# Two steps of a linear-attention round trade places: level product and X-transposed product on TensorE, their sums on VectorE

## What is computed

```python
def step(carry, inp):
    s, mem = carry
    qt, kt, vt, sdt, abt, bbt = inp
    mem = DECAY * mem + sdt
    hard = (mem > THR)                       # spikes; mem is lowered by THR where one fell
    ...
    s = s * alpha[..., None]                 # decay gate, per key channel
    u = jnp.einsum('bhd,bhdv->bhv', kt, s)
    s = s - beta[..., None] * jnp.einsum('bhd,bhv->bhdv', kt, u)
    s = s + beta[..., None] * jnp.einsum('bhd,bhv->bhdv', kt, vt)
    out = jnp.einsum('bhdv,bhd->bhv', s, qt)
    return ((s, mem), out)
...
y = x + y @ w_out * gate
y = y + silu(h2 @ w_ff1) * (h2 @ w_ff3) @ w_ff2
# then cross attention over 77 context rows, and a feed-forward part with signs as weights
```

## Time and profile before

| | |
|---|---|
| median of 3 runs | 1113.32 us (1108.06 to 1115.84) |
| the profiled execution | 1114.58 us, its span 1112.8 us |
| PE busy | 976.0 us (88%) |
| PE weight loads busy | 653.3 us (59%) |
| DVE busy | 699.5 us (63%) |
| ACT busy | 481.1 us (43%) |
| POOL busy | 210.5 us (19%) |

### The profile page before, as it was taken

The page is one execution under the profiler, slowest core; times in us unless marked ns, Lnnn a source line. Parts: engine busy times, 40 slices in busy tenths (PEclk is TensorE's granted clock), DMA queues, the critical chain, the costliest instruction groups (busy, mean ns, idle before and its releaser), DMA issues. The chain is left out here.

```text
span 1112.8 us, 40031 instructions
## 1 busy us (share of the span) xinstructions
PE 976.0 (88%) x16710; PEld 653.3 (59%) x16710; DVE 699.5 (63%) x2510; ACT 481.1 (43%) x1378; POOL 210.5 (19%) x394
## 2 busy tenths in 40 slices
PE   6888769999999999999999888689799899899896
PEld 2332347777777777777777776365446446446442
DVE  2886886988888888889776664146235425524710
ACT  7667312555555555555555555213124323323311
POOL 7100200212222122122122211222101111210300
PEclk8989955999999999999999999789899999899999
DMA  3000000000000000000001000400001000000100
GB/s 95 1 0 1 1 2 3 4 4 4 4 4 4 4 5 4 4 4 5 4 4 29 4 4 4 130 10 23 0 1 29 14 1 21 21 1 4 30 0 10
DMA packets 18652, 13.83 MB, mean 12 GB/s; under 512 B 2491, under 2 KB 17259, under 8 KB 18475
## 3 DMA queue, kind: packets, MB, share of 16 engines
q1 hardware_dynamic: 18475, 11.28, 3.5%
HBM read 7.70 MB, written 1.05 MB: 8 GB/s over the span
## 5 line engine op out<-in xcount | busy, mean ns | idle before, releaser
L935 PE MATMUL banks<-work 64*64 64x64 f32 x3072 | 98.5, 234 | 26.2 <-DVE gates L674 13.0
L994 PE MATMUL banks<-work 64*64 64x32 f32 x2560 | 108.1, 224 | 6.4 <-ACT work L1351 5.0
L1285 ACT COPY work<-banks 128x128 f32<-128x128 f32 x160 | 43.1, 269 | 160.2 <-PE banks L970 160.0
L199 DVE SCALAR_TENSOR_TENSOR gates<-mom,gates 128x16 f32<-128x16 f32 x512 | 100.6, 196 | 9.5 <-ACT gates L1258 4.5
L203 DVE SCALAR_TENSOR_TENSOR mom<-gates 128x16 f32<-128x16 f32 x512 | 102.8, 201 | 5.0
L994 PEld LDWEIGHTS banks<-work 64*64 64x64 f32 x2560 | 92.8, 139 | 19.0 <-issue 10.9
L637 DVE COPY_PREDICATED gates<-work,banks 128x256 f32<-128x256 uint32 x192 | 102.0, 531 | 1.1
L935 PEld LDWEIGHTS banks<-work 64*64 64x64 f32 x3072 | 73.3, 139 | 44.6 <-issue 21.4
L531 POOL TENSOR_TENSOR mom<-mom 128x4 f32<-128x4 f32 x32 | 7.2, 226 | 386.5 <-ACT work L1330 386.5
L608 DVE TENSOR_TENSOR work<-work 128x256 f32<-128x256 f32 x160 | 67.8, 424 | 19.5 <-PE banks L935 18.5
L647 DVE TENSOR_TENSOR work<-work,banks 128x128 f32<-128x128 f32 x160 | 45.6, 285 | 50.1 <-PE banks L994 47.0
(11 more groups left out here) (256 smaller groups left out, 2141.5 us busy)
## 6 DMA issues: line engine op xcount, KB each, us to landing
work<-gates SPq DMA_DIRECT2D x28, 38.5 KB
qT<-in_x_dram SPq DMA_DIRECT2D x4, 256.0 KB, 4.1
work<-in_x_dram SPq DMA_DIRECT2D x4, 256.0 KB, 2.8
out_dram<-work SPq DMA_DIRECT2D x4, 256.0 KB, 2.3
gates<-in_w_ff_dram SPq DMA_DIRECT2D x3, 256.0 KB, 3.4
wv_sb<-in_wv_dram SPq DMA_DIRECT2D x1, 512.0 KB, 5.0
work<-in_w_out_dram SPq DMA_DIRECT2D x1, 512.0 KB, 4.1
gates<-in_x_Wq_dram SPq DMA_DIRECT2D x1, 512.0 KB, 5.4
```

Of the source, the lines that this page charges most:

```text
L199: ve.scalar_tensor_tensor(mem[:, :, t], neg_mem, -0.9, mem[:, :, t], ALU.mult, ALU.add).then_inc(charged, 1)
L935: last = pe.matmul(level_out(l)[to, a], KS[rows, n.two, hp], late[rows, hp], start=True, stop=True)
L994: last = pe.matmul(packed(psXT, l)[rows, a], Z[rows, l - 1, z], second_half(XT[:, n.two], l)[rows, a], start=True, stop=True)
L1285: ac.copy(first_half(Z[:, l - 1], l), packed(psZX_half, l)).then_inc(z_ok, 1)
```

## The change

In four of the five steps of a body, l = 1, 2, 3 and 5, TensorE's `level(aft, l)` goes ahead of `make_xt(nxt, l)`. VectorE's `add_xt(nxt, l)` goes from in front of `prefix(aft, l)` to behind `suffix(aft, l)`, still ahead of `keep(aft, l)`. Step 4 stays as it was. No instruction is added or removed.

```diff
@@ VectorE's body
                         spike(scan, h + 1)
-                        if nxt:
+                        if nxt and l == 4:
                             add_xt(nxt, l)
                         if l == 4 and gate:
                             drive(gate)
@@
                         spike(scan, h + 3)
                         if aft:
                             suffix(aft, l)
+                        if nxt and l != 4:
+                            add_xt(nxt, l)
                         spike(scan, h + 4)
                         if aft:
                             keep(aft, l)
@@ TensorE's body
                         if l == 4 and gate:
                             spike_sums(gate)
-                        if nxt:
+                        if nxt and l == 4:
                             make_xt(nxt, l, gate, gate_old)
                         if l == 4 and gate and gate.n > HP:
                             spike_counts(gate, aft)
                         if aft:
                             level(aft, l, gate, gate_old)
+                        if nxt and l != 4:
+                            make_xt(nxt, l, gate, gate_old)
                         if l == 3 and cur:
                             correct(cur)
```

## The result

| | before | changed |
|---|---|---|
| median | 1110.71 us (4 runs) | 1131.91 us (4 runs, 1127.59 to 1133.49) |
| ratio | | 1.0179, 95% interval 1.0127 to 1.0231 |
| profiled execution, span | 1112.8 us | 1130.9 us |

A forecast was written before the change was run, and what follows sets the result against it. TensorE and VectorE were both nearly full, bound by chains of waits between them. Losses of 7.8 (steps 1 to 3), 4.4 (step 5), 1.4 and 3.0 us (other bodies) sum to 16.6, giving 1130 us; range 1118 to 1140.

The forecast's parts named there:

- The first rival: Waits ahead of `add_xt(1)` and `prefix(5)`: both vanish, 0.57 us off each of 22 bodies, 1101 us; chance 0.07.
- the one that nothing changes: Whole kernel: TensorE overlaps `make_xt` and the level product in either order, 1113 us; chance 0.03.
- Step 1: `level(1)` ahead of `make_xt(1)`: `level(1)` some 0.2 us earlier, `add_xt` takes 0.20 back, `level(2)` gains 0.09 us.
- Step 2: `make_xt(2)` behind `level(2)` loses the wait for `keep(1)` that covered it: `make_z(3)` 0.13 us late.
- Step 3: `make_xt(3)` no longer fills the wait for `beta`: `correct` 0.31 us late in 15 bodies, 0.45 in 7; 7.8 us.
- GpSimd's hold: VectorE's spike held beside GpSimd's `keys`, late by step 1: 0.20 us in 16 of 22 bodies, 1133 us; chance 0.16.
- Step 5: End of body: `add_xt(5)` delays `keep(5)`, and level 0 waits for it: 0.20 us a body, 4.4 us in 22.
- the ring: Level product, `prefix`, `suffix`, `keep`, next level product: said to set the time in steps 1 and 2.
- The side sum for TensorE: End of body: with `make_xt(5)` queued behind `level(5)`, TensorE reaches level 0 at 417.45 instead of 417.35.
- The swallowed lateness: Wait for `alpha` in step 5 absorbs the 0.31 to 0.45 us of steps 1 to 3: 1122 us; chance 0.22.
- The other bodies: Four bodies with gates and no spikes lose 1.4 us in all; five with neither lose 0.6 each, 3.0.
- the upper bound: `make_xt` behind the level product costs its whole 0.63 us: `correct` 0.62 late, 0.96 a body, 1141 us.

The follow-up runs named there:

- step 2 alone: Kernel before with both halves of the change (TensorE's and VectorE's reordering) in step 2 only: 1.0106 of before.
- step 1 alone: Kernel before with both halves of the change in step 1 only: 1.0016 of before, interval holding 1.
- VectorE's half: Kernel before with only `add_xt` moved behind `suffix` in steps 1, 2, 3 and 5, TensorE's order as before: 1.0209 of before.
- the run with `add_xt` behind `keep`: Kernel before with the change in step 5 only, but `add_xt(5)` placed behind `keep(5)`: 1.0005 of before.
- TensorE's half alone: Kernel before with only the level product ahead of `make_xt` in steps 1, 2, 3 and 5, `add_xt` still ahead of `prefix`: 1.0621, 1179.6 us.
- split keys with step 1: Kernel before with GpSimd's `keys` as four instructions of one head pair each, plus both halves of the change in step 1: 1.0029 of before.
- steps 1 to 3: Kernel before with both halves of the change in steps 1, 2 and 3, step 5 as before: 1.0139 of before.
- step 3: Kernel before with both halves of the change in step 3 only: 1.0073 of before.
- step 5 (both ways): Kernel before with the change in step 5 only: `add_xt(5)` ahead of `keep(5)` 1.0042 of before, behind it 1.0005.
- split keys alone: Kernel before with GpSimd's `keys` as four instructions of one head pair each, same result: 0.9965 of before.
- short keys: GpSimd's `keys` computes one head pair of four, output not the reference's: 0.9966 of before in the old order, 1.0138 in the changed order.

## Why the prediction was right

**The sum.** 1130 us were forecast, 1.015 of the median then known; measured are 1131.9 and 1.0179. The rise itself was forecast as 16.6 us; it is 18.1 between the profiled executions and 21.2 between the medians, since the median of before fell to 1110.7 with a fourth execution. That 1130 came so close is in part that luck. The first rival (1101) and the one that nothing changes are out. The order of the parts was right, their sizes partly by luck, as follows.

**Step 1** was right to 0.02 us in the body walked: `level(1)` at 2.73, `keep(1)` at 4.20 (forecast 4.19), `level(2)` at 5.07 (5.06). TensorE's `make_z(2)` was 0.15 us late, not 0.20.

**Step 2** and its lost cover: `make_z(3)` 0.09 to 0.16 us late (forecast 0.13). The run of step 2 alone shows the step to be a loss.

**Step 3** was right in kind and too high for that body, too low for the mean. `correct` was 0.21 us late in the body walked, forecast 0.31: `make_xt` behind the level product took 0.33 us up to `correct`, and only up to `turn_out` the 0.39 of the sum. But most bodies are not that one. I had given 7 of 22 to the wait for `beta`; in the changed kernel the wait is in 13 places. The walk did say that `make_xt` fills the wait for `beta`, but it let `beta` "move little", and in 13 bodies `beta` is late by the hold; without cover all of that lateness comes through. In the mean of the 20 bodies `correct` is 0.46 us late (0.36 by the sum), `alpha` 0.54, and with the 0.20 of step 5 that is the 0.74 us a body, not the 0.55 of the sum: 14.8 us in 20 bodies instead of 11.1. The term of steps 1 to 3 is the one that was mis-sized.

**GpSimd's hold**, the rival of 0.16, came in addition: 13 bodies held ahead of `keep(2)` instead of 6. Its price measured with the short instruction is 0.10 us a body, where the rival had 0.15 (3.3 us over 22). Its path was another: the rival had `keys` late by step 1, but step 1 alone took the hold away from `keep(2)`, and step 2 alone brought it to 11 bodies, since `add_xt(2)` puts the spike inside `keys`.

The rule of the Trainium skill, "SBUF — State Buffer", section "Who interferes with whom", is borne out: what has two inputs in SBUF was held beside `keys` (a spike, and in the run of VectorE's half `suffix`), and what reads PSUM and SBUF was not. The section also says that the order of issue decides which of the two blocks, so that GpSimd can be the one held; the prediction left this out, and the last paragraph of this text has it. In the changed kernel one `add_xt` starts inside `keys` and takes its usual 0.28 us:

```profile
237.19 0.74 POOL L506 TENSOR_TENSOR work<-kT,gates 128x256 f32<-128x256 f32 x1
237.24 0.28 DVE L647 TENSOR_TENSOR work<-work,banks 128x128 f32<-128x128 f32 x1
```

**Step 5** was right: 0.20 us, end 2.05 us, and it is the ring. The side sum for TensorE (417.45) was too high, since it gave `read_chunk` its whole length of 1.05 us; the run with `add_xt` behind `keep` had level 0 start 0.88 us after it.

**The swallowed lateness** (0.22) did not come: `level(5)` is as late as `correct`, in the walked body 0.25 against 0.21 us.

**The other bodies**: with gates alone 1.3 us, forecast 1.4. Without gates 4.3 us in four, where 0.6 each, 2.4, was forecast; the granted clock, next but one section, has part in the excess. **What made the sum come out** is also the start: the two bodies ahead of the first mark were forecast to lose 1.1 us, and the stage was 3.0 us shorter in the profiled execution. That is scatter of single executions as far as the runs show: the first mark lies between 190.6 and 200.4 us in the 14 traces, and in those with the old order in all steps at 193.6, 196.3 and 198.0. Without it the forecast would have been some 4 us further off, still inside the range.

Two smaller slips: at the upper bound `correct` is 0.55 us late by the prediction's own terms (0.31 + 0.24), not 0.62, which moves the 1141 by some 1 us; and the 0.70 for slower is more than the 0.52 and 0.16 that it is made of.

## What to carry to other kernels

A wait that is taken away from one engine can be worth nothing, as here, if the work that stood in another engine's wait loses its place. Ask of each moved step both what it waited for and whose wait it was filling, and put work that nobody waits for behind the step that somebody does: the same `add_xt` cost 0.20 us a body ahead of `keep` and nothing behind it. An order on two engines is one choice, not two: TensorE's half alone cost over three times what both cost together (6.2% against 1.8%), and VectorE's half alone as much as both (2.1%).

## What the runs showed of the hardware

**The granted clock.** TensorE's granted clock has a part in the result, and the prediction had left it out. Stretches of the kernel before (columns as in the earlier trace rows: busy us of PE, PEld, DVE, ACT and POOL; then the granted clock as a share of 2.4 GHz, the DMA share and GB/s):

```profile
180.00:185.00 5.00, 5.00 (x122) 4.13 (x125) 3.12 (x14) 1.11 (x3) 1.18 (x2) 0.50 0.02 3
630.00:640.00 10.00, 8.59 (x317) 6.98 (x312) 7.30 (x23) 4.91 (x21) 3.34 (x9) 1.00 0.02 6
```

The same stretches of the changed kernel:

```profile
180.00:185.00 5.00, 4.51 (x134) 3.54 (x132) 4.96 (x22) 0.90 (x3) 2.49 (x7) 0.91 0.02 3
630.00:640.00 10.00, 8.66 (x265) 6.78 (x266) 6.47 (x21) 3.26 (x17) 3.41 (x9) 0.83 0.01 3
```

And two of split keys with step 1:

```profile
610.00:620.00 10.00, 8.89 (x234) 7.08 (x230) 6.28 (x19) 3.90 (x19) 3.58 (x10) 0.69 0.02 3
630.00:640.00 10.00, 9.38 (x232) 7.77 (x236) 5.56 (x17) 3.13 (x13) 3.98 (x12) 0.66 0.02 5
```

From 180 to 185 us the kernel before ran at 0.50, the lower level of 1.2 GHz, and the changed one at 0.91: the clock had risen earlier there, which fits its shorter start. From 630 to 640 us, in the bodies without gates, the kernel before ran at full clock and the changed one at 0.83. With split keys and step 1 two such stretches stood at 0.69 and 0.66, and two bodies took 17.5 us instead of 15. In the four bodies without gates such falls are seen in the changed kernel, in both halves alone (TensorE's half has these bodies from 657 to 726 us, and 0.80 and 0.85 from 670 to 690), and in steps 1 to 3, step 1, step 2, and split keys with step 1. They are not seen there in the kernel before, nor with step 3, step 5 (both ways), split keys alone, or short keys in either order. From 660 to 690 us every one of the 14 traces has a stretch below 1.00, the kernel before too (0.86 from 660 to 670 us), so the orders differ in when the clock falls and not in whether it does. Earlier falls are in TensorE's half (0.66 from 260 to 270 and from 340 to 350 us) and in one body of step 2. In all kernels with step 1 changed on TensorE, TensorE waits longer for `keep` ahead of `level(1)` in these bodies, where `make_xt(1)` used to stand (0.9 us, 0.4 to 0.5 elsewhere); but in the changed kernel the fall at 633 us follows a body in which that wait was 0.4 us, the changed order with short keys has the long waits and no fall, and VectorE's half and step 2 have falls without them. So what brings the fall is open, and I have not tried it. What it costs can be read only roughly, since the pauses below differ too: in the changed order with short keys, at full clock all through, these bodies take 15.66 us, 0.3 more than the 15.35 of before, and in the changed kernel 16.42.

**TensorE's pauses.** Between the first and the last mark of a body, the 14 traces together have 897 places in which TensorE runs no matmul for more than 0.3 us. For 782 of them the profile names a wait for another engine, for 115 it names none ("issue"). All 115 end 1.2 to 1.7 us after the end of a transfer in the queue "q8 instruction"; of the 782 only 39 do. These transfers are 16 KB each, 105 or 106 between these marks in every kernel however long it takes, one every 4.2 to 5.0 us, so they follow the progress of TensorE, which has by far the most instructions (16710 matmuls and as many weight loads, against 2510 of VectorE). That TensorE stands there for want of its next instructions is the reading that this suggests; no run changed the number of instructions, so it is not tried. How many of the pauses fall where they cost depends on the order: in the 20 bodies with spikes none before, one with the changed order, six with step 1 alone.

**Who is held.** When a spike and `keys` collide, the starts that the profile shows don't say which of them is held, but the length of `keys` does. In the kernel before, ten spikes ahead of `keep(2)` began 0.13 or 0.14 us after `keys`. Six took 0.71 to 0.72 us, and `keys` 0.80 or 0.81; four took 0.18 or 0.19, and then `keys` took 0.91 or 0.92. The three other kernels that keep the old order in steps 1 and 2 (step 3, and step 5 both ways) show the same two pairs in 31 more collisions, 21 against 10, and no third. What decides between them, the traces don't show.
